# Inverting the diagonal blocks in two groups of tiles, with PE's other work beside them and the biases folded into the weights

## The chip, the cores and the metric

The kernel runs on one core of a Trainium2 chip. The metric is the device time of one execution in microseconds (us). The kernel before took 251.79 us (median of 3 runs, 251.52 to 253.14). Engines: PE is TensorE, DVE is VectorE, ACT is ScalarE, POOL is GpSimd, SP is SyncE, which issues transfers. Everything is float32.

## The reference, cut to what matters

The input is x of 4 sequences, 1024 rows, 128 columns. `ln` is a layernorm without gain and bias.

```
h  = ln(x)
a  = ln(h) * dn_g + dn_b
qkv = a @ gates_w + gates_b ; lr = a @ lr_w + lr_b
k  = k / |k|
A  = tril(k k^T, -1) + I              # 1024 x 1024 for each sequence
u  = solve_triangular(A, v, lower)
y  = (q k^T) (lr * u)                 # = q (k^T (lr * u))
h  = h + y @ out_w + out_b
h  = h + relu((ln(h)*mn_g + mn_b) @ w1 + b1) @ w2 + b2
x  = x + h
s  = ln(x)
out = x + s + expert_w[argmax(s @ gate_w^T)] applied to s
```

## The kernel before, in words

A **tile** is 128 consecutive rows of one sequence. t (0 to 7) is the place in the sequence and n (0 to 3) the sequence; the kernel handles the four tiles of one t together. All order is written out by hand: each engine has one list of instructions, with semaphores between them.

**Stage A, projections** (loops at L579, L383, L246, L865). For each t: DVE takes row statistics (`stats`, L551) and scales (`scale`, L559). POOL and ACT each normalise two tiles into `xh` (`xh_`, L221 and L340). PE transposes (`xT_`), ACT writes `xnT_all` with gain and bias (`xnT_`, L348). PE makes keys (`kT_`) and values (`v_`, L845), `k_` transposes the keys back, `gram` forms k k^T. ACT copies keys and products out of PSUM (L354, L358, L368) and DVE adds the value bias (L569). POOL clears `tt_all` for one t (L242) and copies the four 32x32 diagonal blocks of each tile into `gd_all` (`blocks`, L229).

**Stage B, inversion** (L586 to L625, DVE). A 32x32 block transpose brings the diagonal blocks of all 32 tiles to one tile per lane: lane 32b+tile holds block b of that tile. Each lane then inverts its block by 31 elimination steps; step j has a product (L610) and a subtraction (L617) over (31-j) rows of j+1 elements, in two halves where that is large. The two transposes that follow (L622, L623) bring the inverses back. Beside it PE prepares the expert weights (L874 to L891), and ACT forms `h_all` (L370). POOL does nothing in this stretch.

**Joins** (`ya`, `za`, `y64_`, `t12`, from L894). The 128x128 inverse of a tile is put together from its four 32x32 inverses by four rounds of small PE products; each round is copied out of PSUM by ACT or DVE before the next. POOL copies inverses into `tt_all` (`tt_`, L266) and `da` (`da_`, L275). Tiles t=0 and t=1 are joined before the loop of stage D, the others inside it, one t ahead.

**Stage D, recurrence** (L969 and the loops at L447 and L673). For each t and n: `ks` on PE (key times state), `rv_` on DVE, `w_` on PE (solve), copy on ACT, `s_` on PE (state update), `sm` on DVE, `lrw` on ACT, and `m_` on PE, which accumulates one product over all t.

**Stage E, turn** (L991 to L1047). The sum of `m_` is copied (`mT`), multiplied by out_w (`mw`), by a constant for the bias (`cb`, L995) and by `wqT` (`gn`), each with a full copy between; POOL adds `cb` to `h_all` (`hcb_`, L305). Then follow for t=0: `delta`, statistics, `tn`, `tT_`, `hid_`, `out_`, `x1_`, `x1T_`, `gate`.

**Stage F, experts** (L1048). For each t: PE computes all eight experts of t (`experts`, L1028) and the layers of t+1 and t+3; DVE picks by a mask (`pick`, L747).

Of the kernel before, what the change touches and what calls it, by code (L numbers as in the profile page):

```python
# [11 lines left out]
AX_X = mybir.AxisListType.X  # L12
F32 = mybir.dt.float32
# [3 lines left out]
def delta_block_kernel(  # L17
# [11 lines left out]

    NS, L, C = x.shape  # L30
# [3 lines left out]
    TN = T * NS  # L34
    VW = C + 1
    EH = E // 2
    assert C == P and F == P and NS == 4 and TN == Q and E == 8
# [4 lines left out]
    with ExitStack() as ctx:  # L42
# [11 lines left out]
        def rows(t):  # L54
# [5 lines left out]
        epsc = sb("epsc", [P, 1])  # L60
        wq, wqT, wk = sb("wq", [P, C]), sb("wqT", [P, C]), sb("wk", [P, C])
        wvl = sb("wvl", [P, VW])
        bv = sb("bv", [P, C])
        lrb = sb("lrb", [P, 1])
        wo, bo = sb("wo", [P, C]), sb("bo", [P, C])
        w1s, w2s, b2s = sb("w1s", [P, C]), sb("w2s", [P, C]), sb("b2s", [P, C])
        cols = sb("cols", [P, 7])
        dng, dnb, bkc, mng, mnb, b1c, bqc = [cols[:, j:j + 1] for j in range(7)]
        bqB = sb("bqB", [P, P])
# [11 lines left out]
        v_all = sb("v_all", [P, T, NS, C])  # L81
        gg_all = sb("gg_all", [P, T, NS, P])
        tt_all = sb("tt_all", [P, T, NS, P])
        lr_all = sb("lr_all", [P, TN])
        nk_all = sb("nk_all", [P, TN])

# [10 lines left out]

        gd_all = sb("gd_all", [P, Q, TN])
        lt = sb("lt", [P, Q, Q])
        lts = gd_all  # L100
        xi = sb("xi", [P, Q, Q])
        prod = sb("prod", [P, Q * Q])
        rd, nkl = sb("rd", [P, Q]), sb("nkl", [P, Q])
        dT_all = sb("dT_all", [P, Q, TN])
        d_all = sb("d_all", [P, Q, TN])
# [4 lines left out]
        da = [sb(f"da{s}", [P, NS, 2 * Q]) for s in range(2)]  # L110
# [5 lines left out]
        mT, mw, gn, cb = sb("mT", [P, NS, C]), sb("mw", [P, NS, C]), sb("gn", [P, NS, C]), sb("cb", [P, NS, C])  # L116
# [5 lines left out]
        x1T = [v_all[:, 0], v_all[:, 1]]  # L122
        sel = [v_all[:, 2], v_all[:, 3]]
# [4 lines left out]
        k_loaded, v_loaded, g_loaded, w_loaded, e_loaded = (sem("k_loaded"), sem("v_loaded"), sem("g_loaded"),  # L128
                                                            sem("w_loaded"), sem("e_loaded"))
        zeroed, ident_ready, cent_ready, xi_ready, consts_ready, cleared = (sem("zeroed"), sem("ident_ready"), sem("cent_ready"),  # L130
                                                                   sem("xi_ready"), sem("consts_ready"), sem("cleared"))
# [4 lines left out]
        k_mm, k_ready, g_mm, g_ready, gd_done, last_gd = (sem("k_mm"), sem("k_ready"), sem("g_mm"), sem("g_ready"),  # L136
                                                          sem("gd_done"), sem("last_gd"))
        h_ready, xb2_ready = sem("h_ready"), sem("xb2_ready")
        lt_done, rd_done, nkl_done, xi_set, elim = (sem("lt_done"), sem("rd_done"), sem("nkl_done"), sem("xi_set"),
                                                    sem("elim"))  # L140
        dT_done, d_done, nk_done = sem("dT_done"), sem("d_done"), sem("nk_done")
        wT_mm, wT_ready, ewT_mm, ewT_ready = (sem("wT_mm"), sem("wT_ready"), sem("ewT_mm"), sem("ewT_ready"))
        ewC_mm, ewC_ready, bqB_ready = sem("ewC_mm"), sem("ewC_ready"), sem("bqB_ready")
        tt_set, tt_first, da_set = sem("tt_set"), sem("tt_first"), sem("da_set")
        ya_mm, yb_mm, ya_ready, yb_ready = sem("ya_mm"), sem("yb_mm"), sem("ya_ready"), sem("yb_ready")
        za_mm, zb_mm, za_ready, zb_ready = sem("za_mm"), sem("zb_mm"), sem("za_ready"), sem("zb_ready")
        y64_mm, y64_ready, t12_mm, t12_ready = sem("y64_mm"), sem("y64_ready"), sem("t12_mm"), sem("t12_ready")
# [3 lines left out]
        mT_ready, mw_mm, mw_ready, cb_mm, cb_ready, gn_mm, gn_ready = (  # L151
            sem("mT_ready"), sem("mw_mm"), sem("mw_ready"), sem("cb_mm"), sem("cb_ready"), sem("gn_mm"), sem("gn_ready"))
        dl_mm, hcb_ready, h2_ready, xb_ready = sem("dl_mm"), sem("hcb_ready"), sem("h2_ready"), sem("xb_ready")
# [7 lines left out]
        ex_mm, picked, default_set, scaled, added, stored = (sem("ex_mm"), sem("picked"), sem("default_set"), sem("scaled"), sem("added"),  # L161
                                                  sem("stored"))

        last_added = sem("last_added")


        def parts(j):
            m, w = Q - 1 - j, j + 1
# [3 lines left out]
        elim_at = [2 + sum(2 * len(parts(i)) for i in range(j + 1)) for j in range(Q - 1)]  # L172
# [7 lines left out]

        def diagonal(t):
            return t[:, :, :].rearrange("p a b -> p (a b)")[:, 0:Q * Q:Q + 1]

        @block.sync
        def _(sp):
            for t in range(2):
                sp.dma_start(x_all[:, t], x_v[:, t]).then_inc(x_loaded[t], 16)
            for dst, src in ((wvl[:, 0:C], gates_w[:, 2 * C:3 * C]), (wvl[:, C:VW], lr_w),
                             (bv[:, :], gates_b[2 * C:3 * C].partition_broadcast(P)),
                             (lrb[:, :], lr_b.partition_broadcast(P))):  # L190
                sp.dma_start(dst, src).then_inc(v_loaded, 16)
            for t in range(2, T):
                sp.dma_start(x_all[:, t], x_v[:, t]).then_inc(x_loaded[t], 16)
            for dst, src in ((b2s[:, :], b2.partition_broadcast(P)), (wq[:, :], gates_w[:, 0:C]), (wo[:, :], out_w),
                             (w1s[:, :], w1), (w2s[:, :], w2), (bo[:, :], out_b.partition_broadcast(P)),
                             (mng, mn_g.unsqueeze(1)), (mnb, mn_b.unsqueeze(1)), (b1c, b1.unsqueeze(1)),
                             (bqc, gates_b[0:C].unsqueeze(1))):
                sp.dma_start(dst, src).then_inc(w_loaded, 16)
# [13 lines left out]
        def _(pool):  # L212
            nc.gpsimd.memset(ident[:], 0.0).then_inc(zeroed, 1)
            pool.wait_ge(zeroed, 1)
            nc.gpsimd.affine_select(out=ident[:], in_=ident[:], compare_op=ALU.not_equal, fill=1.0, base=0,
                                    pattern=[[-1, P]], channel_multiplier=1).then_inc(ident_ready, 1)
            nc.gpsimd.memset(epsc[:], EPS).then_inc(consts_ready, 1)
            nc.gpsimd.memset(xi[:], 0.0).then_inc(xi_ready, 1)
            nc.gpsimd.memset(cent[:], 1.0 / C).then_inc(zeroed, 1)

            def xh_(t):  # L221
                s = t % 2
                pool.wait_ge(rr_done, t + 1)
# [864 lines left out]
```

## Time and profile before

The profiled execution took 251.73 us, with a span of 249.8 us from the first to the last instruction.

| engine | busy us | share of the span |
|---|---|---|
| PE | 201.3 | 81% |
| DVE | 151.9 | 61% |
| ACT | 120.0 | 48% |
| POOL | 89.7 | 36% |

Busy shares are averages over stages that have different limits, so they are read by stage. The granted clock is a share of TensorE's full speed: 1.00 is 2.4 GHz and 0.50 is 1.2 GHz. A window's mean between the two has some time at each level. In the chain of waits, a row is a piece of the chain that ended last; `x2` is a piece of two instructions.

### The profile page before, as it was taken

Reading aid. Unit: us, or ns where it says so; the run is one execution under the profiler, and the core shown is the slowest. Engines: PE = TensorE matmul, PEld = TensorE weight load, DVE = VectorE, ACT = ScalarE, POOL = GpSimd, SP = SyncE. Lnnn points to the kernel's source line nnn. Section 1 sums busy time; section 2 is a strip of 40 time slices with the busy share of each in tenths; the row PEclk is TensorE's granted clock in tenths of the full one; section 3 lists DMA queues with packets and bytes.
Section 4 is the critical chain, followed back from the end, with each engine's and each line's share of the span. In section 5 each row is a group of like instructions: output and inputs, shape, how many; then the busy total and the mean of one; then the engine's idle time right before and its main releaser. Section 6 shows DMA issues by size and latency. Waiting matters only on the chain.

```text
span 249.8 us, 4068 instructions
## 1 busy us (share of the span) xinstructions
PE 201.3 (81%) x1328; PEld 143.2 (57%) x1328; DVE 151.9 (61%) x626; ACT 120.0 (48%) x316; POOL 89.7 (36%) x146
## 2 busy tenths in 40 slices
PE   0599899570048899999998628899999999999981
PEld 0398777320047888888887426556566655555630
DVE  2648632999961444353452171687879787786875
ACT  2468786839322344344535234535372736564230
POOL 2548888100078606444500280320505143020120
PEclk9999999765555599999999995999999999999998
DMA  5930000000000000000000000000101010110111
GB/s 131 290 96 0 3 3 0 0 0 1 0 3 3 0 0 3 3 0 5 1 3 0 0 0 3 0 0 0 43 3 42 0 42 5 42 42 0 45 42 42
DMA packets 12134, 5.58 MB, mean 22 GB/s; under 512 B 1737, under 2 KB 12113, under 8 KB 12113
## 3 DMA queue, kind: packets, MB, share of 16 engines
q1 hardware_dynamic: 11536, 5.25, 7.5%
q8 instruction: 11, 0.18, 0.3%
q10 hardware_dynamic: 576, 0.07, 0.2%
q14 instruction: 11, 0.08, 0.1%
HBM read 3.22 MB, written 2.10 MB: 21 GB/s over the span
## 4 chain that ended last, share of the span: by engine, by line
PE 60%; DVE 15%; ACT 6%; issue 1%; POOL 0%; DVEq 0%
PE ps L1033 21%; PE ps L831 7%; DVE xi L617 4%; DVE prod L610 4%; PE ps L826 4%; PE ps L947 4%; PE ps L1010 3%; PE ps L955 3%; PE ps L941 3%; PE ps L1025 3%; PE ps L951 2%; PE ps L927 2%; PE ps L935 2%; DVE v_all L760 2%; PE ps L902 2%
## 5 line engine op out<-in xcount | busy, mean ns | idle before, releaser
L1033 PE MATMUL ps<-ewC,v_all 128*128 128x512 f32 x128 | 60.3, 595 | 0.8 <-DVE v_all L760 0.7
L760 DVE COPY_PREDICATED v_all<-mask,ps 128x256 f32<-128x256 int32 x112 | 48.8, 436 | 19.0 <-ACT v_all L504 11.9
L1033 PEld LDWEIGHTS ps<-ewC,v_all 128*128 128x128 f32 x128 | 22.1, 191 | 19.2 <-issue 16.5
L314 POOL TENSOR_TENSOR x_all<-x_all,v_all 128x512 f32<-128x512 f32 x7 | 8.9, 1270 | 58.1 <-ACT v_all L510 58.1
L272 POOL COPY tt_all<-dT_all 32x128 f32<-32x128 f32 x30 | 11.8, 393 | 26.7 <-DVE dT_all L622 24.9
L902 PE MATMUL ps<-tt_all,gg_all 32*32 32x32 f32 x128 | 5.2, 205 | 16.1 <-POOL tt_all L272 16.1
L306 POOL TENSOR_TENSOR h_all<-h_all,cb 128x512 f32<-128x512 f32 x8 | 10.1, 1266 | 19.6 <-DVE cb L689 19.6
L226 POOL TENSOR_SCALAR xh<-x_all,mv,rr 128x128 f32<-128x128 f32 x16 | 12.6, 796 | 9.3 <-DVE rr L561 8.8
L646 DVE TENSOR_SCALAR tt_all<-ps 64x256 f32<-64x256 f32 x8 | 3.3, 417 | 20.6 <-PE ps L935 20.6
L281 POOL COPY da<-d_all 32x128 f32<-32x128 f32 x21 | 8.3, 397 | 20.1 <-PE ps L935 18.8
L569 DVE TENSOR_TENSOR v_all<-ps,bv 128x512 f32<-128x512 f32 x8 | 5.5, 692 | 15.8 <-PE ps L848 15.8
L483 ACT ACTIVATE k_all<-h_all,nb,rr 128x128 f32<-128x128 f32 x32 | 13.7, 483 | 2.8 <-DVE nb L714 2.8
L902 PEld LDWEIGHTS ps<-tt_all,gg_all 32*32 32x32 f32 x128 | 4.3, 117 | 18.0 <-issue 17.2
L310 POOL TENSOR_TENSOR x_all<-x_all,h_all 128x512 f32<-128x512 f32 x8 | 10.2, 1269 | 12.4 <-DVE h_all L694 12.4
L504 ACT COPY v_all<-ps 128x256 f32<-128x256 f32 x16 | 5.8, 366 | 16.3 <-PE ps L1033 16.3
L826 PE MATMUL ps<-ident,xh 128*128 128x128 f32 x32 | 6.0, 317 | 9.5 <-POOL xh L226 9.5
L955 PE MATMUL ps<-k_all,ww 128*128 128x128 f32 x64 | 12.2, 324 | 1.4 <-ACT ww L435 0.7
L372 ACT ACTIVATE h_all<-x_all,nb,rr 128x128 f32<-128x128 f32 x32 | 12.5, 491 | 0.0
L831 PEld LDWEIGHTS ps<-gn,xnT_all 128*128 128x128 f32 x64 | 9.1, 209 | 5.9 <-issue 3.4
L237 POOL COPY gd_all<-gg_all 32x128 f32<-32x128 f32 x28 | 11.3, 404 | 3.2 <-ACT gg_all L368 1.3
L617 DVE TENSOR_TENSOR xi<-xi,prod 128x110 f32<-128x110 f32 (+33 forms) x58 | 12.2, 247 | 0.1
L610 DVE TENSOR_TENSOR prod<-gd_all,xi 128x110 f32<-128x110 f32 (+33 forms) x58 | 12.1, 246 | 0.1
(134 smaller groups left out, 463.8 us busy)
## 6 DMA issues: line engine op xcount, KB each, us to landing
x_all<-in_L_attn_x_dram SPq DMA_DIRECT2D x8, 256.0 KB, 4.6
out_dram<-x_all SPq DMA_DIRECT2D x7, 256.0 KB, 2.3
ew<-in_L_ffn_expert_w_dram SPq DMA_DIRECT2D x1, 512.0 KB
out_dram<-x_all SPq DMA_DIRECT2D x2, 128.0 KB, 1.8
wk<-in_L_attn_gates_w_dram ACTq DMA_DIRECT2D x1, 64.0 KB, 3.8
wvl<-in_L_attn_gates_w_dram SPq DMA_DIRECT2D x1, 64.0 KB, 3.9
bv<-in_L_attn_gates_b_dram SPq DMA_DIRECT2D x1, 64.0 KB, 3.4
b2s<-in_L_attn_b_dram SPq DMA_DIRECT2D x1, 64.0 KB, 4.4
```

The source lines that it names most:

```text
L226: nc.gpsimd.tensor_scalar(xh[s][:, n], x_all[:, t, n], mv[:, 0, t, n, 0:1], rr[:, t, 1, n:n + 1], ALU.subtract, ALU.mult).then_inc(xh_pool, 1)
L272: nc.gpsimd.tensor_copy(tt_all[r, t, :, Q * b:Q * b + Q], dT_all[r, :, t * NS:t * NS + NS].rearrange("p r n -> p n r")).then_inc(tt_set, 1)
L372: last = nc.scalar.activation(h_all[:, t, n], x_all[:, t, n], ACT.Identity, bias=nb[:, t, 0, n:n + 1], scale=rr[:, t, 0, n:n + 1])
L483: nc.scalar.activation(tn[t % 2][:, n], h_all[:, t, n], ACT.Identity, bias=nb2[:, t, n:n + 1], scale=rr2[:, 0, t, n:n + 1]).then_inc(tn_re ...
L610: nc.vector.tensor_tensor(mul[half], lts[:, j, lo:hi].unsqueeze(2).broadcast_to([P, hi - lo, w]), xi[:, j, 0:w].unsqueeze(1).broadcast_to( ...
L617: nc.vector.tensor_tensor(xi[:, lo:hi, 0:w], xi[:, lo:hi, 0:w], mul[half], ALU.subtract).then_inc(elim, 1)
L760: nc.vector.copy_predicated(sel[t % 2][:, n], mask[t % 2][:, n, E - 1 - e].unsqueeze(2).broadcast_to([P, 2, F]), ps[:, b:b + 2, (e % EH) * ...
L826: last = nc.tensor.transpose(tiles(bank)[:, n], src(n), ident[:])
L831: last = nc.tensor.matmul(tiles(bank)[:, n], lhsT(n), rhs(n), start=True, stop=True)
L902: last = nc.tensor.matmul(ps[lo:lo + Q, bank, n * Q:n * Q + Q], gg_all[hi:hi + Q, t, n, lo:lo + Q], tt_all[hi:hi + Q, t, n, hi:hi + Q], st ...
L955: last = nc.tensor.matmul(tiles(4)[:, n], ww[:, n, C:2 * C], k_all[:, t, n], start=t == 0 and n == 0, stop=t == T - 1, skip_group_check=True)
L1033: last = nc.tensor.matmul(ps[:, 4 + 2 * half + n, :], x1T[t % 2][:, 2 * pair + n], ewC[:, EH * half:EH * half + EH, :].rearrange("p e f -> ...
```

## The change: what it does

- The 32 tiles are split into group 0 (t 0 to 3) and group 1 (t 4 to 7). Each group has 16 tiles, and a tile's block now takes two lanes: lane 32b+16q+tile holds the columns of parity q. A step covers (31-j) rows of j//2+1 elements. Both groups are inverted by DVE, one after the other (`invert`).
- Stage A: gain and bias are folded into the key and value weights at the start (`folded`: three products each), so the projection is made from `xh` transposed plus one. DVE clears five t of `tt_all` and POOL three at the start. Statistics come in parts of 1, 1, 2, 2, 2 t. `v_` leaves the loop, `gram` moves ahead of `k_`, and the gram copy is taken before the key copy. POOL copies the diagonal blocks of every t.
- Beside the inversion of group 1: ACT does all the copies of the joins of t=0 to 3; PE's list there has the joins, the values `v_` and six pieces of expert preparation (`prep`) one after another.
- Stage D: the loop of t joins t+4 (so t 0 to 3 join, t 4 to 7 do not). `h_all` is formed here, two tiles each on POOL and ACT.
- Stage E: mT, mw and gn are made in halves (tiles 0, 1 and tiles 2, 3). The output bias is accumulated into gn's PSUM, `cb` and `hcb_` are gone, and t=0 runs through in halves.
- Stage F and the end keep their order; `experts` has one more wait.

```diff
-            for t in range(T):            # POOL, stage A
-                clear(t)
+            for t in range(T):
                 if t + 2 < T:
+                    earlier(pool, gd_done, NB * t)
                     xh_(t + 2)
-                if t < T - 1:
-                    blocks(t)
+                blocks(t)
+            nc.gpsimd.memset(da_all[0:Q, :, :, Q:2 * Q]..., 0.0).then_inc(da_clear, 1)
+            for g in range(NG):
+                pool.wait_ge(dT_done, g + 1)
+                for b in (1, 3):
+                    nc.gpsimd.tensor_copy(by_block(tt_all, g, r, b), dT_all[g][r]).then_inc(tt_pool, 1)
+                nc.gpsimd.tensor_copy(by_block(da_all, g, r, 1), plain(g)[r]).then_inc(tt_pool, 1)
...
+            for g in range(NG):           # DVE
+                invert(g)
+            def invert(g):
+                dve.wait_ge(gd_done, NB * TG * (g + 1))
+                earlier(dve, nkl_done, g)
+                nc.vector.transpose(lt, gd[g] twice side by side)
+                nc.vector.reciprocal(rd[:], diagonal(lt))
+                nc.vector.tensor_tensor(lts[:], lt[:], rd..., ALU.mult)
+                for q in range(2):
+                    nc.vector.tensor_scalar(diagonal of xi[g] of parity q, rd[:, q:Q:2], pm[:, q:q + 1], None, ALU.mult)
+                for j in range(Q - 1):
+                    w, halves = j // 2 + 1, parts(j)
+                    for half, lo, hi in halves:
+                        nc.vector.tensor_tensor(mul[half], lts[:, j, lo:hi]..., xi[g][:, j, 0:w]..., ALU.mult)
+                    for half, lo, hi in halves:
+                        nc.vector.tensor_tensor(xi[g][:, lo:hi, 0:w], xi[g][:, lo:hi, 0:w], mul[half], ALU.subtract)
+                nc.vector.transpose(d_all[g] <- xi[g])
+                nc.vector.transpose(dT_all[g] <- plain(g))
...
+            v_(0); v_(1); prep(0); v_(2); prep(1); ya(0); v_(3)     # PE, beside the inversion
+            for t in range(TG):
+                za(t)
+                prep(2 + t)
+                y64_(t)
+                if t + 1 < TG:
+                    ya(t + 1)
+                else:
+                    v_(T - 1)
+                t12(t)
+                if t + 1 < TG:
+                    v_(TG + t)
+            nkl_(1)                       # ACT, after its copies for the list above
+            diagonals(1)                  # three copies of 32x512
...
             for t in range(T):            # stage D, PE (ACT and DVE alike)
-                joins = 0 < t < T - 1
+                joins = t + TG < T
                 if t > 0: ks(t, n) for all n
                 if joins:
-                    ya(t + 1)
+                    ya(t + TG)
...
+            act.wait_ge(m_mm, 1)          # stage E
+            for of in (LOW, HIGH):
+                nc.scalar.copy(mT[:, span(of)], tiles(4)[:, span(of)]).then_inc(mT_ready, 1)
-            nc.tensor.matmul(ps[:, 6, :], bqB[:], rows(mw[:, :, :]), start=True, stop=True).then_inc(cb_mm, 1)
+            delta(0, LOW); delta(0, HIGH, 3); delta(1)
+            tT_(0, LOW); hid_(0, LOW); tT_(0, HIGH, 6); out_(0, LOW); hid_(0, HIGH, 7)
+            x1T_(0, LOW); out_(0, HIGH, 7); delta(2); gate(0, LOW); experts(0, 0, 0)
+            x1T_(0, HIGH, 6); gate(0, HIGH)
```

(Some lines are shortened to their operands; the wait lines that only follow from the order are left out.)

## Rows read from the trace of the kernel before

**Rows 1.** Busy by stage: window, length, busy (instructions) of PE, PEld, DVE, ACT, POOL, clock, DMA, GB/s
```profile
0.00:44.56 44.56, 33.99 (x217) 28.24 (x218) 22.38 (x115) 28.14 (x59) 30.76 (x64) 1.00 0.29 73
44.56:71.10 26.54, 7.87 (x26) 3.51 (x24) 26.16 (x123) 16.21 (x43) 1.49 (x4) 0.61 0.00 0
71.10:82.10 11.00, 8.13 (x108) 6.92 (x103) 3.41 (x12) 2.31 (x8) 9.47 (x21) 0.50 0.01 3
82.10:137.40 55.30, 53.15 (x576) 46.28 (x576) 22.18 (x78) 24.13 (x88) 19.29 (x36) 0.95 0.01 2
137.40:157.90 20.50, 12.26 (x55) 8.59 (x55) 7.74 (x29) 7.47 (x16) 8.18 (x7) 0.83 0.00 1
157.90:236.30 78.40, 78.40 (x343) 47.00 (x344) 60.60 (x242) 39.52 (x96) 19.29 (x16) 1.00 0.07 21
```

**Rows 2.** Timeline of POOL in stage A: start us, us, instruction
```profile
17.63 1.80 POOL L237 COPY gd_all<-gg_all 32x128 f32<-32x128 f32 x4 [1.05 <-ACT gg_all L368]
28.47 1.57 POOL L226 TENSOR_SCALAR xh<-x_all,mv,rr 128x128 f32<-128x128 f32 x2
30.17 1.80 POOL L237 COPY gd_all<-gg_all 32x128 f32<-32x128 f32 x4
32.02 0.53 POOL L242 MEMSET tt_all<- 128x512 f32 x1
34.34 1.79 POOL L237 COPY gd_all<-gg_all 32x128 f32<-32x128 f32 x4
```

**Rows 3.** Busy by window, columns as in Rows 1: one t of stage A
```profile
30.17:34.34 4.17, 3.74 (x27) 3.07 (x28) 2.77 (x15) 3.19 (x7) 3.71 (x8) 1.00 0.00 0
```

**Rows 4.** Chain of waits: start us, us, piece; the values of t=7, then the inversion
```profile
41.28 0.89 PE ps L848 x8
...
44.56 1.25 DVE lt L595
46.22 1.23 DVE gd_all L600
48.06 0.23 DVE prod L610
48.89 0.24 DVE xi L617 x2
53.94 0.38 DVE xi L617 x2
```

**Rows 5.** Timeline of DVE and POOL in stages E and F: one operation twice
```profile
146.35 0.69 DVE L714 SCALAR_TENSOR_TENSOR nb<-mv,rr 128x4 f32<-128x4 f32 x1
171.77 0.15 DVE L714 SCALAR_TENSOR_TENSOR nb<-mv,rr 128x4 f32<-128x4 f32 x1
145.75 1.26 POOL L306 TENSOR_TENSOR h_all<-h_all,cb 128x512 f32<-128x512 f32 x1
```

**Rows 6.** Busy by window, columns as in Rows 1: around PE's pause
```profile
57.00:70.00 13.00, 0.00 (x0) 0.00 (x0) 12.86 (x65) 8.58 (x23) 0.52 (x2) 0.51 0.00 1
82.00:88.00 6.00, 5.89 (x27) 5.90 (x28) 2.10 (x8) 2.34 (x8) 3.65 (x7) 0.50 0.00 0
88.00:96.00 8.00, 7.75 (x94) 6.67 (x93) 3.45 (x13) 3.26 (x12) 0.54 (x2) 1.00 0.01 2
```

**Rows 7.** Chain of waits in stage D: `ya` of two neighbouring t, `ks` of the last t
```profile
96.36 0.52 PE ps L902 x16
103.96 0.52 PE ps L902 x16
...
133.26 1.09 PE ps L941 x8
```

**Rows 8.** Chain of waits in stage E: `tn`, `hid_`, then `delta(2)` and `out_(0)`
```profile
147.07 1.66 ACT k_all L483 x4
...
150.29 2.08 PE ps L1010 x2
152.37 3.43 PE ps L831 x16
```

More of the change, by code:

```diff
@@ L370, in h_, with v_ @@
[L370 to L374 removed]
+                nc.scalar.copy(rows(gg_all[:, t]), ps[:, 2 + t % 2, :]).then_inc(g_ready, 1)
+            def v_(t):
+                b = 2 * (t % 2)
+                act.wait_ge(v_mm, t + 1)
+                nc.scalar.copy(v_all[:, t].rearrange("p (b n) c -> p b (n c)", b=2), ps[:, b:b + 2, 0:2 * VW]).then_inc(v_ready, 1)
@@ L633, in yb @@
+            nc.vector.memset(prod[:], 0.0).then_inc(cleared, 1)
+            dve.wait_ge(cleared, 1)
+            for g in range(NG):
+                invert(g)
+            for g in range(NG):
+                dve.wait_ge(nkl_done, g + 1)
+                nc.vector.transpose(nk[g][:], nkl[g][:]).then_inc(nk_done, 1)
             def yb(t):
@@ L892, in _, with v_ @@
-            pe.wait_ge(ewC_ready, 1)
-            pe.wait_ge(g_ready, T)
+                four(2 + t % 2, lambda n: kT_all[:, t, n], lambda n: kT_all[:, t, n], g_mm)
+            def v_(t):
+                earlier(pe, v_ready, t - 1)
+                for n in range(NS):
+                    last = nc.tensor.matmul(ps[:, 2 * (t % 2) + n // 2, VW * (n % 2):VW * (n % 2) + VW], xnT_all[:, t, n], wvc[:],
+                                            start=True, stop=True)
+                last.then_inc(v_mm, 1)
@@ L1016, in x1T_ @@
-            def x1T_(t):
-                pe.wait_ge(x1_ready, t + 1)
-                pe.wait_ge(tT_ready, t + 1)
-                turn(1, lambda n: x_all[:, t, n], x1T_mm)
-            def gate(t):
-                pe.wait_ge(x1T_ready, t + 1)
-                earlier(pe, mask_ready, t)
-                for n in range(NS):
+                    t12(t + TG)
+            pe.wait_ge(w_loaded, 16 * 8)
+            for bank, of in ((7, LOW), (3, HIGH)):
+                nc.tensor.matmul(rows(tiles(bank)[:, span(of)]), oner[:], bor[:, :].unsqueeze(1).broadcast_to([1, 2, C]),
+                                 start=True, stop=False)
@@ new lines, in _, with delta @@
+            for pair, of in enumerate((LOW, HIGH)):
+                pe.wait_ge(mT_ready, pair + 1)
+                four(5 + pair, lambda n: mT[:, n], lambda n: wo[:], mw_mm, of)
+            for pair, (bank, of) in enumerate(((7, LOW), (3, HIGH))):
+                pe.wait_ge(mw_ready[pair], 1)
+                nc.tensor.matmul(rows(tiles(bank)[:, span(of)]), wqT[:], rows(mw[:, span(of)]), start=False,
+                                 stop=True).then_inc(gn_mm, 1)
+            def delta(t, of=ALL, bank=0):
+                earlier(pe, h2_ready, NS * t if t > 1 else 2 * t)
+                four(bank, lambda n: xnT_all[:, t, n], lambda n: gn[:, n], dl_mm, of, len(of))
@@ new lines, in tT_, with hid_ @@
+            def tT_(t, of=ALL, bank=1):
+                pe.wait_ge(tn_ready, upto(t, of))
+                earlier(pe, x1T_ready, NS * t)
+                turn(bank, lambda n: tn[t % 2][:, n], tT_mm, of, len(of))
+            def hid_(t, of=ALL, bank=2):
+                pe.wait_ge(tT_ready, upto(t, of))
+                earlier(pe, x1_ready, NS * t)
+                nc.tensor.matmul(rows(tiles(bank)[:, span(of)]), w1s[:], rows(tT[t % 2][:, span(of)]), start=True,
+                                 stop=True).then_inc(hid_mm, len(of))
```

946 lines of the change are left out of this document (493 added, 453 removed).

## The prediction

> **What bounds the kernel now.** I read busy time by stage first, because the kernel's stages have different limits [rows 1]. Stage A lasts 44.6 us with every engine partly busy. In stage B DVE works 26.2 of 26.5 us: nothing but the inversion matters there, and PE waits at 1.2 GHz. The joins of t=0 and 1 take 11.0 us at 1.2 GHz. The recurrence (55.3 us) and the experts (78.4 us) are PE's: 53.2 and 78.4 us busy. The turn between them, 20.5 us, is a chain of waits in which no engine is busy throughout. I then read POOL's timeline and one t of stage A [rows 2, 3]: the diagonal copies of two neighbouring t start 4.17 us apart, and POOL is busy 3.71 us of that, more than its share in the page suggests. Third come the steps of the inversion in the chain [rows 4], and then what PE's clock does around a pause [rows 6].
>
> **Stage A and the first inversion.** POOL loses the clearing, 0.53 us for each t; PE loses the values, 0.89 us (8 products) [rows 2, 4]. ACT's 3.19 us and POOL's 3.71-0.53 are then nearly equal [rows 3]; with the waits between them I take 3.6 us for each t. The weights must be folded before the first key product, about 0.7 us later than now (my estimate for one larger weight transfer on ACT's queue, two scalings and three products in series; SP's queue now issues all of x before anything else, which helps t=2), but the statistics of t=2 no longer stand behind the values, so the first diagonal copy moves from 17.6 to about 16.1 us (it waited for POOL and DVE in turn, not for data). Three t later plus its own 1.8 us, group 0 is ready at 16.1+10.8+1.8=28.7 us. It may be 28 to 32: the start is a chain over four engines. DVE's five clearings stand ahead of the first statistics, while it waits for x; if that cover is gone they cost up to 2 us.
>
> **One group of the inversion.** A step is two instructions, or two pairs. A pair of 45 and 42 elements takes 0.24 us, one of 121 and 110 takes 0.38 us [rows 4]: 0.156 us plus 0.97 ns for an element. A single small one takes 0.23 us. With j//2+1 columns a group has 31 steps with 2856 elements (before: 5456): 23 steps in two halves with 2534 elements, 46 pairs by 0.156 plus 2x2534x0.97 ns, that is 7.2+4.9=12.1 us, and 8 single steps by 0.47, 3.8 us: 15.9 us. Ahead of it stand the transpose and the scaling (1.25 and 1.23 us, both still full size) and 0.7 us of small ones; behind it two transposes of half size, 1.8 us. Sum 20.9 us. Two groups cost 41.8 us where one pass took 26.5: halving a step does not halve its price, and the gain can come only from starting earlier and from what lies beside the second group.
>
> **The port.** All steps of the inversion read two operands from SBUF. In the kernel before POOL is silent in stage B (1.5 us busy [rows 1]); now group 0 is inverted while POOL still copies the diagonals of t 4 to 7 and normalises t=7. What happens then is seen once clearly: a 4-element operation with two SBUF inputs takes 0.15 us alone and 0.69 us beside POOL, and it ends as POOL's 1.26 us do [rows 5]. So I charge POOL's time to DVE: 16 copies of 0.45 and two normalisations of 0.78 are 8.8 us, less about 0.1 us for each of 18 in which DVE's issue overlaps and less POOL's own gaps: 6.4 us. The bounds are 0 and 8.8. The Trainium skill says the same with a reason (SBUF — State Buffer, "Who interferes with whom"): a Vector instruction with two SBUF inputs and a GpSimd one that reads SBUF exclude each other for the whole instruction. By that rule POOL is held up too, and the loss could reach the 8.8 us or move to stage A; this trace agrees for DVE and shows nothing for POOL.
> Group 0 then ends at 28.7+20.9+6.4=56.0 us. POOL's three copies of 32x512 have no row: from the cleared 128x512 (0.53) to four of 32x128 (1.80) [rows 2]; I take 1.2, since a copy of 128 elements is at 0.45 and a 512-element sum at 1.26 [rows 5]. With 0.6 us of waiting for DVE's scaling, the first join can start at 56.0+3.6+0.6=60.2 us.
>
> **Beside the second group.** Two joins took 11.0 us at 1.2 GHz with 8.1 us of PE work, 5.5 each [rows 1]; at 2.4 GHz 3.5 us are left. In PE's list each also carries one value step (0.89 us and ACT's copy) and one preparation; all preparation was most of 7.9 us at mostly 1.2 GHz [rows 1], nearly 2 us for each of the last two at full clock, partly beside ACT's copies. I take 4.3, 4.3, 4.9 and 4.9 us at 2.4 GHz, plus 4.4 us because PE comes out of a pause: 22.8 us, until 83.0. ACT's three copies of group 1 and a root stand behind that, 2.1 us: the recurrence's list can begin at 85.1 us. The other path is shorter: the second group, delayed some 2.4 us by POOL's three copies, ends at 56.0+20.9+2.4=79.3, and POOL's copies at 82.9. The joins set the time, by 2 us.
>
> **Recurrence.** A t with a join takes 7.60 us, the last one, without, 4.14 (133.26 to 137.40) [rows 1, 7]. Now four join, the first of them without `ks` (-1.1), and four do not: 4x7.6-1.1+4x4.1=45.7 us, plus 3.3 for the first 6 us at 1.2 GHz, as now [rows 6]. The new `h_all` (two of about 0.49 on ACT, three POOL operations) lies beside PE: ACT is busy 24 of 55 us [rows 1]. The last one is not covered, 0.5 us. The end comes at 85.1+49.0=134.1 us, 3.3 us before 137.4.
>
> **Turn.** The halves take away whole copies between products; the longest pieces are `tn` (1.66), `hid_` at 1.2 GHz (2.08) and `delta(2)` with `out_(0)` (3.43) [rows 8]. Followed through in halves, the first gate comes 14 us after the recurrence instead of 20.5. But the warm clock at 157.9 came from the dense work just before; the same 6 us at 1.2 GHz will now fall in stage F and cost up to 3 us. I count 16.2 with the 0.5 above, a gain of 4.3 (bounds 2 and 7). Stage F and the end stay: PE is busy all through [rows 1], and what POOL loses there was hidden.
>
> **Sum.** 3.3+4.3=7.6 us. The profiled execution took 251.73 us with a span of 249.8; it is 0.06 below the median, so no correction: **244 us**, with 240 to 249 for this case. About 1% (2.5 us) is what a measurement of this kernel can tell from no change.
>
> **Rivals.**
> 1. *DVE and POOL do not get in each other's way.* Then 6.4+0.6 us come back and the joins still set the end (78.1 against 74.3+3.6): 237 us. For it: the stall is seen on operations of few elements only. Against: [rows 5]. Chance 0.2.
> 2. *PE stays at 1.2 GHz through the four joins: slower.* PE pauses from about 50 to 60 us, and its clock falls in a pause [rows 6]. From 70 to 82 us it worked 8.6 of 12 us in small products and was not raised; only the dense stretch from 82 raised it at 88. If the mixed list is as little use as those joins, they take 22.8+12=35 us (5.5 each plus the values and preparation at half speed), and the result is 256 us. It decides from 30.4 us on, where the gain of 7.6 is used up. For it: that stretch; against: the list now has values and expert products in between, and at 1.2 GHz it leaves PE hardly any pause. Chance 0.15. The Trainium skill describes such a pattern (TensorE: Matmul & The Clock Gate, "HAM oscillation"): work in bursts between waits starts at the low clock every time. By it this rival would be the forecast; [rows 6] agree for one pause each.
> 3. *The two-lane steps are no shorter than before.* If a step has a floor at its present mean of 0.67 us, the 23 long ones cost 15.4 instead of 12.1 us. The change would then not do what it is laid out for: 3.3 us later in group 0, and 247 us. Against: 0.24 against 0.38 us [rows 4]. Chance 0.1.
> 4. *POOL is starved by DVE instead.* Group 0 then ends at 49.6, but blocks and normalisation follow it, and the joins start at 61: 245 us, inside the forecast.
>
> **How the numbers follow.** Forecast with 4: 0.5; the rest, 0.05, is small terms that cancel. Faster by over 1% (below 249.3): 0.48 of the forecast, 0.2 of rival 1 and 0.08 of rival 3, 0.77 with a little of the rest. Slower (above 254.3): 0.11 of rival 2. Within: 0.12. The range of 235 to 254 takes in rival 1 down to its warm-clock end and stops short of rival 2 in full.
>
> **What would show it.** In the trace after: the first DVE transpose of stage B near 29 us; steps of group 0 that stretch to a POOL instruction's end while group 1's late steps do not; dT of group 0 near 56 us; the first join near 60 and ACT's copies of group 1 near 83; 7.6 and 4.1 us for a t; the first gate 14 us after the last `m_`. I am wrong if the inversion's steps run free beside POOL, if the clock rises late in the joins, or if DVE's second group ends after the joins.

## The result, and the profile after

The kernel after took 265.84 us (median of four executions) beside 252.43 us of the kernel before: ratio 1.053, 95% interval 1.047 to 1.058. Forecast were 244 us and a range of 235 to 254. Disturbed executions stand well above the others of their kernel and enter no ratio: one of 650.91 us here beside three from 265.40 to 266.11, one of 1095.1 us of e4_fill_joins, the longer and profiled ones of e3_fill_loop and e6_root_first, and two of e11_shift_again (251.31 and 253.63). The profiled execution took 266.11 us with a span of 264.3; for the kernel before these were 251.73 and 249.8.

The stages of the kernel after, by window: length, busy (instructions) of PE, PEld, DVE, ACT, POOL, then clock, DMA share, GB/s.

```profile
0.00:32.91 32.91, 21.91 (x107) 16.32 (x108) 15.71 (x98) 20.91 (x46) 19.46 (x44) 1.00 0.38 95
32.91:57.99 25.08, 12.60 (x87) 9.51 (x85) 24.33 (x118) 12.97 (x26) 14.12 (x24) 0.86 0.00 1
57.99:89.80 31.81, 28.73 (x278) 22.75 (x279) 19.58 (x119) 15.31 (x41) 3.82 (x5) 0.66 0.01 1
89.80:153.30 63.50, 62.84 (x465) 57.71 (x465) 20.52 (x68) 27.98 (x96) 19.72 (x21) 0.61 0.00 1
153.30:170.00 16.70, 13.09 (x66) 9.38 (x66) 9.06 (x34) 7.70 (x21) 4.50 (x5) 0.90 0.01 1
170.00:264.30 94.30, 86.69 (x354) 49.99 (x352) 70.34 (x275) 41.85 (x104) 15.80 (x13) 0.97 0.08 23
```

The fourth row is the result. The recurrence took 63.5 us where it took 55.3 before [rows 1], although four of its t instead of six have a join. PE was busy 62.8 of the 63.5 us, at a mean clock of 0.61. The chain of waits shows each t of it (start us, us, piece); the first two rows are the first and the last of four `ya` in the list beside group 1, the next three are `ya` in the recurrence, and the last is `w_` of t=4, the first t without a join.

```profile
57.99 0.84 PE ps L975 x16
...
79.55 0.52 PE ps L975 x16
...
89.80 0.84 PE ps L975 x16
101.81 0.80 PE ps L975 x16
113.79 0.80 PE ps L975 x16
...
137.73 1.71 PE ps L1059 x8
```

A t with a join in it (a joined t) lasts 11.98 us (101.81 to 113.79); before it lasted 7.60 [rows 7]. PE's clock by window in the kernel after (window, length, PE busy, clock, DMA share, GB/s):

```profile
58.00:75.00 17.00, 16.86 (x172) 0.50 0.01 2
75.00:80.00 5.00, 5.00 (x46) 0.66 0.00 0
...
86.00:90.00 4.00, 1.05 (x15) 0.83 0.00 0
90.00:110.00 20.00, 20.00 (x158) 0.50 0.01 2
...
130.00:138.00 8.00, 8.00 (x43) 0.50 0.00 1
138.00:146.00 8.00, 8.00 (x62) 0.88 0.01 2
```

The clock rose near 78, during two pairs of 128x512 products of `prep(4)`, and fell in a pause of 2.9 us before 89.80, in which PE waits for ACT's three copies of group 1. Then PE worked without a gap from 90 to 138 at 1.2 GHz, and the clock rose only when t=4 came, the first t that has no join. In the kernel before, the first t of the loop has no join; there the clock was back within 6 us [rows 6].

The start was late as well. ACT in stage A of the kernel after (start us, us, instruction, what ended the wait):

```profile
7.90 0.40 ACT L371 ACTIVATE gall<-wall,cols 128x128 f32<-128x128 f32 x1 [2.87 <-DMA ball<-in_L_attn_gates_b_dram]
...
8.52 1.28 ACT L338 ACT_TABLE_LOAD   x1
9.81 0.21 ACT L338 ACTIVATE sd<-ab 128x8 f32<-128x8 f32 x1
```

The first root runs at 9.81 us, behind the weights' transfer, their scaling and a second table load. DVE's inversion in the kernel after, group 0 and then group 1:

```profile
32.91 1.25 DVE L649 STREAM_TRANSPOSE lt<-gd 128x1024 f32<-128x1024 f32 x1 [2.35 <-POOL gd L269]
...
36.16 0.29 DVE L670 TENSOR_TENSOR prod<-lts,xi 128x31 f32<-128x31 f32 x1
...
53.22 1.03 DVE L683 STREAM_TRANSPOSE d_all<-xi 128x512 f32<-128x512 f32 x1
...
56.87 2.06 DVE L654 TENSOR_TENSOR lts<-lt,rd 128x1024 f32<-128x1024 f32 x1
59.25 0.19 DVE L670 TENSOR_TENSOR prod<-lts,xi 128x31 f32<-128x31 f32 x1
...
74.89 1.04 DVE L683 STREAM_TRANSPOSE d_all<-xi 128x512 f32<-128x512 f32 x1
```

The steps of group 0, beside POOL (busy 8.8 us in that stretch), took 36.16 to 53.22, 17.06 us; those of group 1, without POOL, 59.25 to 74.89, 15.64 us.

### The profile page after: what moved, and what is told of

The parts are those of the page before. It is cut to its first block, busy times and chain, and to the rows that moved or that the text cites. A ratio compares the mean times of both kernels' runs of the same rounds, so it can differ in the third digit from the quotient of the medians.

```text
span 264.3 us, 4252 instructions
## 1 busy us (share of the span) xinstructions
PE 225.9 (85%) x1351; PEld 165.7 (63%) x1351; DVE 159.5 (60%) x709; ACT 126.7 (48%) x332; POOL 77.4 (29%) x110
## 4 chain that ended last, share of the span: by engine, by line
PE 70%; DVE 11%; issue 3%; ACT 2%; POOL 2%; DVEq 0%; POOLq 0%; ACTq 0%
PE ps L1145 21%; PE ps L907 6%; PE ps L1067 5%; PE ps L1059 5%; PE ps L1063 4%; PE ps L1053 4%; PE ps L902 3%; DVE prod L670 3%; DVE xi L677 3%; PE ps L933 3%; PE ps L1120 3%; PE ps L1000 3%; PE ps L1009 3%; PE ps L1136 2%; PE ps L975 2%
## 5 line engine op out<-in xcount | busy, mean ns | idle before, releaser
L1145 PE MATMUL ps<-ewC,kT_all 128*128 128x512 f32 x128 | 60.9, 599 | 0.9 <-DVE kT_all L823 0.8
L823 DVE COPY_PREDICATED kT_all<-mask,ps 128x256 f32<-128x256 int32 x112 | 48.9, 437 | 19.0 <-ACT kT_all L558 11.4
L1145 PEld LDWEIGHTS ps<-ewC,kT_all 128*128 128x128 f32 x128 | 22.3, 192 | 19.5 <-issue 19.5
L670 DVE TENSOR_TENSOR prod<-lts,xi 128x60 f32<-128x60 f32 (+14 forms) x108 | 19.4, 214 | 0.6
L677 DVE TENSOR_TENSOR xi<-xi,prod 128x60 f32<-128x60 f32 (+14 forms) x108 | 19.4, 214 | 0.5
L269 POOL COPY gd<-gg_all 32x128 f32<-32x128 f32 x32 | 14.1, 441 | 6.5 <-ACT gg_all L362 4.5
L311 POOL TENSOR_TENSOR x_all<-x_all,h_all 128x512 f32<-128x512 f32 (+1 forms) x9 | 10.3, 1146 | 18.8 <-DVE h_all L754 11.8
L259 POOL TENSOR_SCALAR xh<-x_all,mv,rr 128x128 f32<-128x128 f32 x16 | 12.6, 797 | 9.0 <-DVE rr L630 8.5
L1059 PE MATMUL ps<-rv,tt_all 128*128 128x128 f32 x64 | 13.8, 383 | 0.0
L558 ACT COPY kT_all<-ps 128x256 f32<-128x256 f32 x16 | 5.8, 364 | 16.1 <-PE ps L1145 16.1
L300 POOL TENSOR_SCALAR h_all<-x_all,mv,rr 128x128 f32<-128x128 f32 x16 | 12.5, 793 | 0.1
L1059 PEld LDWEIGHTS ps<-rv,tt_all 128*128 128x128 f32 x64 | 12.2, 276 | 0.3
L933 PE MATMUL ps<-wvc,xnT_all 128*128 128x129 f32 x64 | 11.8, 344 | 0.3 <-ACT gg_all L362 0.3
```

What stands on the lines that cost most here:

```text
L259: nc.gpsimd.tensor_scalar(xh[s][:, n], x_all[:, t, n], mv[:, 0, t, n, 0:1], rr[:, t, 1, n:n + 1], ALU.subtract, ALU.mult).then_inc(xh_pool, 1)
L269: nc.gpsimd.tensor_copy(gd[t // TG][r, :, t % TG * NS:t % TG * NS + NS].rearrange("p c n -> p n c"), gg_all[r, t, :, Q * b:Q * b + Q]).the ...
L670: nc.vector.tensor_tensor(mul[half], lts[:, j, lo:hi].unsqueeze(2).broadcast_to([P, hi - lo, w]), xi[g][:, j, 0:w].unsqueeze(1).broadcast_ ...
L677: nc.vector.tensor_tensor(xi[g][:, lo:hi, 0:w], xi[g][:, lo:hi, 0:w], mul[half], ALU.subtract).then_inc(elim, 1)
L823: nc.vector.copy_predicated(sel[t % 2][:, n], mask[t % 2][:, n, E - 1 - e].unsqueeze(2).broadcast_to([P, 2, F]), ps[:, b:b + 2, (e % EH) * ...
L933: last = nc.tensor.matmul(ps[:, 2 * (t % 2) + n // 2, VW * (n % 2):VW * (n % 2) + VW], xnT_all[:, t, n], wvc[:], start=True, stop=True)
```

## The experiments

**The theory.** Once the clock is low, a list of joined t does not bring it back, however busy PE is. In them products of 32x32 and 64x64 stand between the 128x128 ones. A t without a join, which has 128x128 products alone (called dense here, as are the 128x512 ones), does bring it back. The kernel before had one in first place; the change put it in fifth. **The rivals.** The pause before the recurrence is to blame, or the mixed list beside group 1 is, or the late start and the port are.

The times of all kernels, with ratios to the kernel before on the same chip:

| kernel | us, median | ratio, 95% interval |
|---|---|---|
| after | 265.84 | 1.053, 1.047 to 1.058 |
| e1_shift | 246.5 | 0.972, 0.963 to 0.981 |
| e11_shift_again (the same kernel) | 247.19 | 0.975, 0.970 to 0.979 |
| e2_before_join0 | 277.22 | 1.093, 1.084 to 1.102 |
| e3_fill_loop | 257.61 (profiled) and 248.92 | |
| e4_fill_joins | 265.38 (profiled) and 1095.1 | |
| e5_prep_first | 248.8 | 0.978, 0.961 to 0.995 |
| e6_root_first | 252.96 (profiled) and 244.92 | |
| e7_group0_alone | 257.94, one run | |
| e8_turn_fill | 245.6 | 0.966, 0.953 to 0.978 |
| e9_all_before_joins | 240.46 | 0.950, 0.945 to 0.954 |
| e10_all_and_root_first | 239.86 | 0.947, 0.944 to 0.951 |
| e12_all_before_no_shift | 257.24 | 1.019, 1.014 to 1.024 |

**e1_shift: one t without a join ahead of the joined ones.** From the kernel after, on PE, ACT and DVE alike:

```diff
             for t in range(T):
-                joins = t + TG < T
+                joins = 0 < t <= TG
 ...
-                    ya(t + TG)
+                    ya(t + TG - 1)
```

> The kernel after, with the joins of group 1 one t later: t=1 to 4 join t+3, so that t=0 has no join. Clock theory (at 1.2 GHz a t with a join does not raise TensorE's clock, a dense t without one does, and once up it holds): t=0 runs at 1.2 GHz in 6 to 8 us, the clock is 1.00 soon after, the joined t take 7.6 us instead of 12.0, total 249 us (244 to 254). Rival (the recurrence with its new list is slow by itself: h_all on POOL and ACT, or the port): joined t stay near 12 us wherever they stand, total 262 us or more.

It took 246.5 us, 19 us less than the kernel after. `ya` in the recurrence of e1_shift (timeline), and then its windows:

```profile
92.46 0.59 PE L975 MATMUL ps<-tt_all,gg_all 32*32 32x32 f32 x16
100.06 0.59 PE L975 MATMUL ps<-tt_all,gg_all 32*32 32x32 f32 x16
```

```profile
85.00:90.00 5.00, 3.16 (x28) 1.00 0.01 3
90.00:110.00 20.00, 19.76 (x246) 1.00 0.01 2
```

A joined t is at 7.60 us again. The first `w_` starts at 87.91 and the last `m_` ends at 133.86: 46.0 us. One thing is mixed here: t=0 no longer waits for ACT's copies of group 1, so the pause shrank from 2.9 to 1.4 us and the clock never fell. That missed the expectation that t=0 would run at 1.2 GHz. The next kernels separate the two.

**e2_before_join0: the same order put into the kernel before.** The loop joins t+2 from t=0 on, on all three engines:

```diff
-                joins = 0 < t < T - 1
+                joins = t < T - 2
 ...
-                    ya(t + 1)
+                    ya(t + 2)
```

> The kernel before, with the joins inside the recurrence one t earlier: t=0 to 5 join t+2 instead of t=1 to 6 joining t+1. Same work, no other change. Clock theory: the clock stays at 0.50 through six joined t of about 12 us each, total 276 us (270 to 282). Rival (list of the changed kernel, not the clock, is to blame): joined t stay at 7.6 us, total 251 to 254 us.

It took 277.22 us, 24 us more than the kernel before, with nothing else changed. Its windows:

```profile
85.00:120.00 35.00, 35.00 (x248) 0.50 0.00 1
120.00:155.00 35.00, 35.00 (x251) 0.50 0.01 2
155.00:170.00 15.00, 10.79 (x68) 0.98 0.00 0
```

PE was busy 70 of 70 us at 1.2 GHz; the clock rose at t=6, the first t without a join. DVE beside POOL in the inversion, the list beside group 1 and the folded biases are not in this kernel, and the pause that PE has before its recurrence is no longer than in the kernel before.

**e3_fill_loop: dense products ahead of the recurrence of the kernel after.** Their result is not used.

```diff
             pe.wait_ge(v_ready, T)
+            for _ in range(4):
+                nc.tensor.matmul(ps[:, 4, :], ident[:], rows(kT_all[:, 0]), start=True, stop=True)
             for t in range(T):
```

> The kernel after, with four 128x512 products that nobody uses in TensorE's list between the last join beside the inversion and the recurrence (extra work, in the pause of 2.9 us). Clock theory: the clock does not fall at 89 us, joined t take 7.6 us from the first, total 248 us (245 to 252). Rival (joined t with this list are slow at any clock, or cannot hold the clock): 264 us or more.

The two executions took 257.61 and 248.92 us (expected 248). In the profiled one the clock did not come up in the list ahead, and the four products began at 92.39 and took 6.05 us at 1.2 GHz; the windows show what followed:

```profile
80.00:92.00 12.00, 12.00 (x79) 0.50 0.00 0
92.00:98.00 6.00, 6.00 (x12) 0.56 0.01 3
98.00:110.00 12.00, 11.88 (x150) 1.00 0.01 1
```

Four dense products raised the clock, and the joined t behind them kept it, at 7.60 us each (`ya` at 98.37 and 105.97). So the joined t are able to hold a high clock, and no run shows them raising it. In this trace the list ahead has the same `prep(4)` and `prep(5)` as in the kernel after (L962 and L964, from 74.82 and from 84.50 us, some 3.7 us each at 1.2 GHz), and the clock stayed at 0.50 through both.

**e4_fill_joins: dense products in the pause ahead of the list beside group 1.**

```diff
             prep(1)
+            for _ in range(9):
+                nc.tensor.matmul(ps[:, 7, :], ident[:], rows(kT_all[:, 0]), start=True, stop=True)
             ya(0)
```

> The kernel after, with nine 128x512 products that nobody uses in the pause from 50 to 58 us ahead of the first join. Clock theory: the four joins run at 2.4 GHz and end near 79 instead of 87 us; the recurrence's list then waits for group 1's inverses (near 80 us), and the total is 258 us if the clock falls in that wait and 242 us if it does not. Rival (the joins are bound by waits between PE and ACT, not by the clock): the joins still end after 85 us.

It took 265.38 us: nothing gained. Its windows:

```profile
57.00:67.00 10.00, 9.59 (x156) 1.00 0.01 3
67.00:80.00 13.00, 13.00 (x99) 0.51 0.01 2
...
89.00:110.00 21.00, 20.84 (x160) 0.50 0.00 1
```

The first joins ran at 2.4 GHz, 3.7 us from one `ya` to the next (57.15, 60.85). Then the clock fell near 67, although PE had been busy 9.59 of the 10 us before and had no wait above 0.26 us. That missed what was expected: none of the outcomes named there had the clock fall without a pause. The list ended at 86.2 us, the time that the rival gave, but not for the rival's reason, since the first joins were short. The dense `prep(4)` and `prep(5)` followed at 68.64 and 78.33 us, 3.7 us each, and did not raise the clock, which in the kernel after `prep(4)` did. The recurrence began at 1.2 GHz again, and its joined t took 12.0 us.

**e5_prep_first: the preparation out of the list.** From e1_shift: the pieces `prep(2)` to `prep(5)` are issued before the first join.

```diff
             prep(1)
+            for j in range(2, 6):
+                prep(j)
             ya(0)
 ...
-                prep(2 + t)
```

> e1_shift with the four later pieces of expert preparation (prep 2 to 5) ahead of the first join, in TensorE's pause from 50 to 58 us, and no longer between the joins. Clock theory: the pause is filled by 6 us of dense products, so the first joins start at 2.4 GHz; with 5 us less between them the last join ends near 80 instead of 86.6 us, total 241 us (238 to 244). Rival (group 1's inversion or ACT's copies set the start of the recurrence): less than 2 us gained, total 245 to 247 us.

It took 248.8 us, no gain where 5 us were expected. The list was no shorter: `nk` of group 1, which stands behind it, starts at 87.12 us in both kernels. PE stayed at 0.50 to the end of it, because the dense pieces that raised the clock near 78 were gone. It also settles what e1_shift left mixed. Its windows:

```profile
84.00:90.00 6.00, 4.62 (x25) 0.50 0.01 3
90.00:110.00 20.00, 19.77 (x217) 0.92 0.00 1
```

The recurrence began at 87.91 us at 1.2 GHz, and t=0, which has no join, raised the clock by itself.

**e6_root_first: the first root ahead of the scaling of the weights.** From e1_shift:

```diff
+            root(0)
+            xh_(0)
             act.wait_ge(g_loaded, 16 * 4)
             act.wait_ge(consts_ready, 1)
             nc.scalar.mul(gall[:, C:2 * C], wall[:, C:2 * C], dng)
             nc.scalar.mul(bmean[:], dnb.broadcast_to([P, P]), 1.0 / C).then_inc(scaled_w, 1)
-            root(0)
-            xh_(0)
```

> e1_shift with ACT's first root and normalisation ahead of the two scalings of weights. Theory for the late start of stage B (the first root stood behind the scalings, which waited for the bias row until 7.9 us, and behind a second table load of 1.28 us): root at 6 instead of 9.8 us, one table load, group 0 ready 1.5 to 3 us earlier, total 244.5 us. Rival (the folding products on TensorE set the start of the first key product): stage B starts within 0.5 us of e1_shift, total 246 us.

The two executions took 252.96 and 244.92 us, too far apart to tell 1.5 us. ACT's order in the trace is plain (timeline of e6_root_first):

```profile
3.69 1.28 ACT L338 ACT_TABLE_LOAD   x1 [3.69 <-issue]
5.98 0.21 ACT L338 ACTIVATE sd<-ab 128x8 f32<-128x8 f32 x1 [1.01 <-DVE ab L624]
```

One table load instead of two, the first root 3.3 us earlier than in e1_shift (9.30), and stage B begins at 30.86 instead of 32.49: of 3.3 us, 1.6 remain, since the second root waits for the weights now (10.74). Whether they reach the end is e10's question.

**e7_group0_alone: group 0 inverted when POOL is silent.** From e1_shift; DVE waits for the blocks of all t, which delays all that follows.

```diff
             def invert(g):
-                dve.wait_ge(gd_done, NB * TG * (g + 1))
+                dve.wait_ge(gd_done, NB * T)
```

> e1_shift in which the inversion of group 0 starts only when all of POOL's diagonal copies are done, so no step runs beside POOL. Port theory: the 31 steps of group 0 take 15.6 us as group 1's do, against 17.1 us beside POOL; the stretching of 1.5 us is all that POOL costs them. If the steps still take 17 us, the stretching has another cause. The total is some 11 us longer (257 us).

Steps of group 0 in e7_group0_alone (timeline of DVE, first step and end):

```profile
47.51 0.19 DVE L670 TENSOR_TENSOR prod<-lts,xi 128x31 f32<-128x31 f32 x1
...
63.13 1.03 DVE L683 STREAM_TRANSPOSE d_all<-xi 128x512 f32<-128x512 f32 x1
```

From the first step to the first transpose that is 15.62 us alone. In e1_shift, beside POOL, it is 17.06 us (35.75 to 52.81), as in the kernel after: POOL costs these steps 1.4 us. Group 0 began 11.8 us later than in e1_shift (44.29 instead of 32.49) and the kernel took 257.94 us, 11.4 more: the date of group 0 passes almost in full to the end.

**e8_turn_fill: dense products in the turn.** From e1_shift, four products of 128x512, unused: two before `tT_(0, LOW)`, one before `hid_(0, LOW)`, one before `tT_(0, HIGH, 6)`.

> e1_shift with four 128x512 products that nobody uses in TensorE's pauses of the turn (two after delta(1), one each after tT_(0) and hid_(0) of the first half). Clock theory (the turn gained less than reckoned because the clock falls in it and is low at the start of stage F): the clock stays at 1.00 from 135 us on, from the end of the recurrence to the end of the span 107.5 instead of 110.4 us, total 243.5 us. Rival (the turn is bound by ACT's and DVE's chain, whatever the clock): 110 us or more, total 246.5 us or more.

It took 245.6 us beside e1_shift's 246.5. The expected rise of the clock came, the gain of 3 us did not. Windows of e8_turn_fill (in e1_shift the clock was 0.80 from 140 to 145, 0.52 from 145 to 150 and 1.00 from 150 to 160):

```profile
140.00:145.00 5.00, 4.93 (x17) 1.00 0.00 0
...
150.00:160.00 10.00, 8.51 (x35) 0.83 0.00 0
```

The first gate came 14.3 us after the last `m_` instead of 16.2, but then the clock fell between 150 and 160, and the gate of t=1 came after 29.5 instead of 29.7 us. The fall is only moved.

**e9_all_before_joins: all values and preparation ahead of the joins.** From e1_shift: `v_(0)` to `v_(7)` and `prep(0)` to `prep(5)` are issued in turn before `ya(0)`, on PE and ACT (new lines drawn together).

```diff
             v_(3)
+            prep(2); v_(4); prep(3); v_(5); prep(4); v_(6); prep(5); v_(7)
+            ya(0)
             for t in range(TG):
                 za(t)
-                prep(2 + t)
                 y64_(t)
                 if t + 1 < TG:
                     ya(t + 1)
-                else:
-                    v_(T - 1)
                 t12(t)
-                if t + 1 < TG:
-                    v_(TG + t)
```

> The kernel of e1_shift, with all eight values v_ and all six pieces prep issued before the first join, so that the list of the four joins holds joins alone. In e1_shift PE was busy 5.00 of 5 us at 1.2 GHz in most windows from 60 to 80 us, with values and preparation a good part of it; in e5_prep_first, where only the preparation had left the list, PE was busy 4.34 of 5 us at 1.2 GHz and the list ended no earlier. Theory A (beside group 1, PE's list is bound by the amount of PE's work at 1.2 GHz): four joins alone cost 5.5 us each as the pair before did, 22 us from 57.5, so the list ends near 79.5 instead of 86; group 1's nk is then there and the recurrence starts near 82, with t=0 unjoined raising the clock: 5 us less than e1_shift, 241 us (239 to 244). Theory B (the list is bound by the joins' rounds over ACT, and the dense pieces only filled PE's waits): no gain, 246 to 248 us, since the dense pieces no longer raise the clock near 78.

It took 240.46 us, some 6.5 less than e1_shift beside it (247.19) and 5% less than the kernel before. The second and third `ya` of the list, the first `w_`, and two `ya` of the recurrence (timeline of e9):

```profile
62.61 0.87 PE L978 MATMUL ps<-tt_all,gg_all 32*32 32x32 f32 x16
67.29 0.87 PE L978 MATMUL ps<-tt_all,gg_all 32*32 32x32 f32 x16
...
79.76 2.04 PE L1065 MATMUL ps<-rv,tt_all 128*128 128x128 f32 x8 [1.47 <-DVE rv L720]
86.02 0.59 PE L978 MATMUL ps<-tt_all,gg_all 32*32 32x32 f32 x16
93.61 0.59 PE L978 MATMUL ps<-tt_all,gg_all 32*32 32x32 f32 x16
```

The joins still run at 1.2 GHz, but from the second `ya` to the third it is 4.68 us instead of 6.70 (63.52 to 70.22 in e1_shift), as PE's values and preparation (2.0 and 0.6 to 3.4 us for each join there) have moved to 42 to 57 us, where PE was busy 6.0 of 15 us in e1_shift and 14.1 at 2.4 GHz in e9. The first join comes 1.7 us later (59.27 instead of 57.58), and the list from there to its last product is 9.9 us shorter (19.0 instead of 28.9). `nk` of group 1 starts at 78.88 instead of 87.12. The recurrence starts at 1.2 GHz, t=0 raises the clock, and the joined t take 7.6 us. From the first `w_` to the end of the last `m_` (127.42) it is 47.7 us.

**e10_all_and_root_first** is e9 with the edit of e6.

> e9_all_before_joins with the first root and the first normalisation on ACT ahead of the scaling of the weights (as in e6_root_first, whose stage B began 1.6 us earlier). If the start of stage A is on the path that sets the end, 1 to 1.6 us less than e9: 240 us (237.5 to 243.5). Rival: ACT's and PE's extra work before the first join now ends later than the first inversion, or the turn's clock moves against it: no difference from e9.

It took 239.86 us (239.47 to 240.79) beside 240.46 (239.46 to 240.94): no difference that six executions of each can tell. Stage B began at 30.77 instead of 31.51 and the first join at 58.53 instead of 59.27, but the clock now fell before 60, the first join took 3.82 instead of 3.34 us, and the first `w_` came at 79.56 instead of 79.76.

**e11_shift_again** is the kernel of e1_shift, on the chip of e9 and e10.

> e1_shift once more, with five rounds, as the reference of this call: 246.5 us again (245.5 to 247.5).

It took 247.19 us.

**e12_all_before_no_shift: the list of e9 with the recurrence of the kernel after.** From e9, the edit of e1_shift undone.

> The kernel after, with all values and preparation ahead of the joins as in e9_all_before_joins, but with the recurrence as in the kernel after (t=0 to 3 join t+4). The list of the joins should end near 78.5 us again, 8 us earlier than in the kernel after. Theory A (a recurrence that begins at 1.2 GHz with a joined t stays there, whatever stood before it): ya(4) near 82 us, joined t of 12.0 us at clock 0.50, the clock up only near 130, when t=4 has no join; the end 8 us before the kernel after's, 258 us (256 to 260), 17.5 us above e9. Rival (the long stay at 1.2 GHz came from the list before it, or from the 3.4 us pause): the clock rises within 6 us as in e9, joined t of 7.6 us, 243 us.

It took 257.24 us. Timeline of e12, `ya(4)` and `ya(5)`, and its windows:

```profile
81.14 0.84 PE L978 MATMUL ps<-tt_all,gg_all 32*32 32x32 f32 x16 [2.95 <-ACT da_all L422]
...
93.08 0.87 PE L978 MATMUL ps<-tt_all,gg_all 32*32 32x32 f32 x16
```

```profile
90.00:110.00 20.00, 20.00 (x158) 0.50 0.00 1
110.00:127.00 17.00, 17.00 (x117) 0.50 0.00 1
```

PE was busy 37 of 37 us at 1.2 GHz. The clock is at 0.50 before the recurrence in e9 and in e12 (0.50 in 78 to 84 us in both), so the fall in the pause is not what sets them apart: it is what comes first in the recurrence, or the longer pause that goes with it (2.95 instead of 1.47 us). In e2_before_join0 the clock stayed low without such a pause (PE's last waits there are 0.46 us and less), which speaks against the pause.

With e12 the four cases are complete: 265.8 us (after), 257.2 (list sorted), 246.5 to 247.2 (recurrence sorted), 240.5 (both). Sorting the recurrence is worth 17 to 19 us, sorting the list 7 to 9, and neither depends much on the other.

## Why the prediction was wrong

The forecast in spans is 242.1 us (244 less the 1.93 outside the span); the kernel after has 264.3, 22.2 more. By the forecast's own dates: `ya(4)` at 89.8 instead of 85.1, +4.7; the recurrence 63.5 instead of 49.0, +14.5; from its end to the end 111.0 instead of 108.0, +3.0.

**The step that failed** is "plus 3.3 for the first 6 us at 1.2 GHz, as now [rows 6]". It took from the kernel before that the clock comes back in 6 us and did not ask what PE does in these 6 us. There it is `w_`, `s_` and `m_` of a t without a join and the `ks` of the next; in the kernel after the first t is joined, and the clock came back after 48 us. Shown by e1_shift, by e2_before_join0 in the other direction, and by e12 beside e9. With the order right the term was too large: the recurrence took 46.0 us in e1_shift, where the clock never fell, and 47.7 in e9, where it began at 1.2 GHz, so the start at the low clock was worth 1.7 us. The rows that warned were quoted in rival 2: 8.6 of 12 us in small products that did not raise the clock. I used them for the list beside group 1 and not for the place where the same joins stand some 30 us later. The change moved a t without joins from first to fifth place, and that was in the diff.

**Stage A and the start: 28.7 forecast, 32.9 measured.** The 0.7 us for the folding was 4 us at the first root, 9.81 instead of 5.83: the wait for the bias row's transfer and the second table load of 1.28 us had no term. The rate after that was right: the first diagonal copy starts at 20.14 (forecast 16.1), and from there to the end of group 0's copies it is 12.7 us (forecast 12.6). With the root ahead of the scaling, 1.6 of 3.3 us reached stage B in e6, and in e10 0.7, of which nothing could be told at the end.

**One group: right.** 20.9 us forecast; in e7, without POOL, from the first transpose at 44.29 to the end of `dT_all`, 20.9 us; the steps 15.6 (forecast 15.9). Rival 3 is out: the steps are as short as their elements say.

**The port: the mechanism right for long operations, wrong for the steps.** Forecast 6.4 us between bounds of 0 and 8.8, measured 1.4. The row that I leaned on [rows 5] shows a short DVE operation held up by one long POOL operation that was already running. Here POOL's copies are 0.44 us and DVE's steps 0.2 us, and POOL's 8.8 us and the 15.6 that the steps take alone fit into 17.06 us: for some 7 us both worked at once. Where one side is long, the other does wait: POOL's four copies beside DVE's 1.22 us `lts` took 2.84 instead of 1.78 us,

```profile
31.02 1.78 POOL L269 COPY gd<-gg_all 32x128 f32<-32x128 f32 x4
...
34.59 2.84 POOL L269 COPY gd<-gg_all 32x128 f32<-32x128 f32 x4
```

(timeline of POOL in the kernel after), and the second `lts` took 2.06 us beside POOL's copy of 32x512 (56.82 to 57.84 us). The Trainium skill (SBUF — State Buffer, "Who interferes with whom") has an exclusive lock for a whole instruction, which goes to whichever engine issued first. These two rows agree with it; the short steps do not, since by it the two could not have worked at once, and there the measurement decides. Rival 1 described group 0 best. The error was not without effect, since e7 shows the date of group 0 in the total. It was hidden: stage A ended 4.2 us late, the port cost 5.0 us less than forecast and the copies behind group 0 1.5 us less (2.7 instead of 4.2), so that the first join came at 57.99 us, near the forecast of 60.2, by luck.

**Beside the second group: 22.8 forecast, 28.9 measured.** The first join came 2.2 us ahead of its date; this list with ACT's copies behind it (2.9 instead of 2.1) cost 6.9 us, which leaves the 4.7. My 4.4 us for coming out of a pause assumed one pause; the clock stayed at 0.50 until `prep(4)` near 78. Rival 2 had 35 us at this place. It was too high, since those dense pairs did raise the clock in the kernel after; in e4 and in the trace of e3 the same pieces did not, and why is open. The Trainium skill (TensorE: Matmul & The Clock Gate, "HAM oscillation — how this bites in real kernels") ascribes a low clock to waits between bursts. The trace agrees for PE's pauses before 58 and before 89.8; the 48 us after that have no waits that could be the cause, so the rule does not cover them.

**Recurrence at full clock: right.** Joined t 7.60 and unjoined 3.94 us (forecast 4.1); the new `h_all` cost nothing visible.

**Turn: the first gate 15.1 us after the last `m_` (forecast 14), the gain 1.4 instead of 4.3.** At the first gate 5.4 us were gained (20.5 before); at the gate of t=1, 30.3 us after the last `m_` (31.9 before), 1.6 were left, because the clock fell between (0.83 in 170 to 180 us). The forecast says up to 3 us for that, and its 16.2 us hold 1.7 of them (16.2 less 14 and 0.5); the two gates differ by 3.8. e8 shows that the fall moves with the work and is not bought off.

## What to carry to other kernels

When a change reorders PE's work, ask of each stretch that begins at the low clock what comes first in it; a joined list that can hold a clock of 2.4 GHz may be unable to raise it, and the dense t ahead of it decided here over everything behind. A dense piece is no guarantee either: `prep(4)` raised the clock in the kernel after and not in e4_fill_joins. Busy time does not show this: the bad recurrence has PE at 99%. And dense work that stood in a list at 1.2 GHz took nearly twice as long there as in the pause ahead of it at the full clock (a value step 2.09 instead of 1.16 us); moving it there took 9.9 us off the list and delayed its start by 1.7 (e9).

## What was not expected of the hardware

- PE ran at 1.2 GHz for 48 us in the kernel after and for 70 us in e2_before_join0 while the profile records it as busy throughout, in t with products of 32x32 and 64x64 between those of 128x128. Why is open: the trace does not show what the chip counts.
- The clock can fall without a pause: in e4_fill_joins near 67 us, after 9.59 busy of 10 us, in a stretch of joins with values. Why is open too.
- Dense work does not raise it each time: `prep(4)` at 75.56 us did in the kernel after, the same piece in e4_fill_joins did not (68.64 to 72.35 us at 0.50).
- A scaling ahead of the first root cost a second table load here: 1.28 us in the kernel after, none in e6_root_first.
